# TensorE's scores moved behind the transposes in odd steps, and the additions at the end shared between two engines

## The reference

```python
h = silu(x @ W1.T + b1) @ W2.T + b2          # x: (16, 256, 128)
qkv = h @ Wg.T + bg                          # 16 heads of 64
dots = einsum('bhid,bhjd->bhij', q, k) * 64 ** -0.5
dots = where(j >= i + 64, -inf, dots)        # keys up to 63 ahead of the query
attn = softmax(dots)
out = einsum('bhij,bhjd->bhid', attn, v) -> (b, n, 1024)
x = layernorm(x + out @ Wo.T + bo)
# then: mixture of 16 experts (4 per token), add, layernorm
#       second attention (16 heads of 8), add, layernorm
#       recurrence: c = f*c + i*g over the 32 steps of 128 x 128
#       h = tanh(x @ wo.T + c_final @ uo.T + bo)
x = layernorm(x + h)                         # the end
```

## Time and profile before

| | |
|---|---|
| median of three runs | 1412.11 us |
| the profiled execution's own time | 1409.84 us |
| its span | 1408.1 us |
| mean granted TensorE clock | 0.968 |
| first attention, from the first scores to the last position | 34.3 to 669.2 us |
| experts | about 683 to 960 us |
| second attention with the recurrence | about 960 to 1379 us |
| the end (additions, norm, stores) | about 1379 to 1408 us |

### The profile page before, as it was taken

The page is one execution under the profiler, slowest core; times in us unless marked ns, Lnnn a source line. Parts: engine busy times, 40 slices in busy tenths (PEclk is TensorE's granted clock), DMA queues, the critical chain, the costliest instruction groups (busy, mean ns, idle before and its releaser), DMA issues.

```text
span 1408.1 us, 36750 instructions
## 1 busy us (share of the span) xinstructions
PE 1259.8 (89%) x9756; PEld 969.6 (69%) x9756; DVE 1016.9 (72%) x3767; ACT 928.8 (66%) x2827; POOL 774.5 (55%) x983
## 2 busy tenths in 40 slices
PE   7999999999999999995799999898687878888883
PEld 3777777777777777764699999896355555556652
DVE  1677777777777777775677777577687878878845
ACT  5877777777777877773456656464466666666554
POOL 1557777777777777775331131215446777764232
PEclk9999999999999999998799999999799999999997
DMA  9622222211222222221122222323232232323102
GB/s 338 222 61 77 74 74 74 63 46 47 74 71 71 74 74 74 74 76 46 53 71 76 80 84 81 88 78 83 62 82 70 68 84 60 88 54 75 40 2 60
DMA packets 149016, 110.98 MB, mean 79 GB/s; under 512 B 12833, under 2 KB 137249, under 8 KB 148770
## 3 DMA queue, kind: packets, MB, share of 16 engines
q1 hardware_dynamic: 139842, 92.45, 22.6%
q0 software_dynamic: 8192, 16.79, 4.4%
q10 hardware_dynamic: 864, 0.39, 0.1%
HBM read 47.27 MB, written 61.93 MB: 78 GB/s over the span
## 4 chain that ended last, share of the span: by engine, by line
PE 24%; DMA 12%; SPq 8%; DVE 5%; issue 2%; ACT 1%; DVEq 1%; ACTq 0%; POOL 0%; POOLq 0%
PE psum L917 8%; PE psum L928 8%; DMA qst<-qkd 6%; SPq L454 3%; DMA wall<-qkd 3%; DMA qkd<-parts 3%; SPq L439 2%; SPq L456 1%; PE psum L1029 1%; PE psum L905 1%; DVE parts L1603 1%; PE psum L941 1%; DVE mx L1536 1%; PE psum L981 1%; PE psum L982 1%
## 5 line engine op out<-in xcount | busy, mean ns | idle before, releaser
L555 POOL TENSOR_SCALAR P<-P,rinv 128x192 f32<-128x192 f32 (+1 forms) x384 | 309.2, 817 | 152.2 <-DVE rinv L1361 149.3
L1166 ACT ACTIVATE P<-shifted,least 128x192 f32<-128x192 f32 (+1 forms) x512 | 240.3, 471 | 107.9 <-DVE least L1345 104.6
L1188 ACT ACTIVATE hid<-psum,wA 128x128 f32<-128x128 f32 x576 | 164.5, 368 | 119.5 <-PE psum L917 119.5
L1536 DVE TENSOR_REDUCE mx<-psum 128x2 f32<-128x512 f32 x256 | 164.5, 686 | 42.1 <-PE psum L1029 34.1
L599 POOL DMA_INDIRECT yk<-xs,posc x128 | 125.0, 977 | 104.7 <-DVE wA L1497 55.4
L1196 ACT ACTIVATE wall<-psum 128x1024 f32<-128x1024 f32 x128 | 130.6, 1020 | 78.1 <-PE psum L941 77.3
L1345 DVE CUSTOM_DVE_ANT_0 shifted<-psum,band 128x192 f32<-128x192 f32 (+1 forms) x512 | 168.5, 384 | 13.1 <-PE psum L804 12.9
L917 PE MATMUL psum<-xgT,wA 128*128 128x128 f32 x1152 | 155.0, 278 | 0.6 <-DVE xgT L1504 0.6
L928 PE MATMUL psum<-wB,hid 128*128 128x128 f32 x1152 | 152.6, 276 | 0.0
L841 PEld LDWEIGHTS psum<-ident,P 128*128 128x128 f32 x1024 | 117.6, 142 | 40.1 <-issue 29.7
L917 PEld LDWEIGHTS psum<-xgT,wA 128*128 128x128 f32 x1152 | 142.8, 195 | 1.3 <-issue 0.7
(11 more groups left out here) (262 smaller groups left out, 2558.0 us busy)
## 6 DMA issues: line engine op xcount, KB each, us to landing
xs<-zrow SPq DMA_DIRECT2D x34, 1024.0 KB, 8.8
xg<-xs SPq DMA_DIRECT2D x144, 64.0 KB
xs<-yrow SPq DMA_DIRECT2D x144, 64.0 KB
wall<-in_wall SPq DMA_DIRECT2D x1, 8232.0 KB, 35.9
qkd<-parts SPq DMA_DIRECT2D x64, 96.0 KB
kst<-qkd SPq DMA_DIRECT2D x22, 128.0 KB
qst<-qkd SPq DMA_DIRECT2D x22, 128.0 KB
wall<-qkd SPq DMA_DIRECT2D x20, 128.0 KB
```

Of the source, the lines that this page charges most:

```text
L555: g.tensor_scalar(x, x, rinv[:, par, n:n + 1], None, ALU.mult).then_inc(s["pn_ready"], 1)
L1166: last = sc.activation(P[:, par, it, h, 0:w], shifted[:, par, it, h, 0:w], ACT.Exp, scale=-1.0, bias=least[:, par, n:n + 1], accum_out=row ...
L1188: sc.activation(hid[:, n % 4, f, :], up(n, f), ACT.Gelu, bias=wA[:, n % 4, F + f:F + f + 1]).then_inc(s["hid_ready"], 1)
L1536: v.tensor_reduce(out=mx[:, :, h], in_=SB[(par + 1 + h) % 3].rearrange("q (i n) -> q i n", i=TT), axis=mybir.AxisListType.X, op=ALU.max).t ...
```

## The change

In TensorE's loop the scores become a function `attend(b, p)`. In even steps it stands where it stood, first in the step. In odd steps it stands behind the transposes (and, in step 5, behind the router products), right ahead of the products with the values. No instruction is added or removed there. At the end GpSimd adds the second half of each group (`add_half`), VectorE keeps the first half; VectorE takes statistics of the first four tiles, then waits for `half_added`, then of the other four.

```diff
@@ GpSimd, the end
+            def add_half(c):
+                pool.wait_ge(s["h_act"], 2 * c + 2)
+                x, h = x_all[:, 8 * c + 4:8 * c + 8, :], xo_all[:, 8 * c + 4:8 * c + 8, :]
+                g.tensor_tensor(x, x, h, ALU.add).then_inc(s["half_added"], 1)
+
+            add_half(0)
             for c in range(GROUPS):
+                if c + 1 < GROUPS:
+                    add_half(c + 1)
                 pool.wait_ge(s["var3_ready"], c + 1)
@@ TensorE, body(b)
+            def attend(b, p):
+                need(pe, "q_ev", pair(b, p, 1))
+                need(pe, "k_ev", pair(b, p, 1))
+                need(pe, "shifted_ready", 4 * pair(b, p))
...
                 for p in range(8):
-                    if is_pair(b, p, 0):
...
+                    if p % 2 == 0 and is_pair(b, p, 0):
+                        attend(b, p)
                     if is_pair(b, p, 7):
                         qk(b, p, pair(b, p, 7))
...
                         last.then_inc(s["m_l"], 1)
+                    if p % 2 == 1 and is_pair(b, p, 0):
+                        attend(b, p)
                     if p % 2 == 1 and is_pair(b, p, -2):
@@ VectorE, squared(c)
-                for half in range(2):
-                    dve.wait_ge(s["h_act"], 2 * c + half + 1)
-                    v.tensor_tensor(x[:, 4 * half:4 * half + 4, :], ...)
+                dve.wait_ge(s["h_act"], 2 * c + 1)
+                v.tensor_tensor(x[:, 0:4, :], x[:, 0:4, :], h[:, 0:4, :], ALU.add)
                 v.drain()
-                moments(v, x, 8, st2, mv2[:, c], nh2[:, c, :], ve2[:, c, :]).then_inc(s["var3_ready"], 1)
+                statistics(v, x, 4, st2)
+                dve.wait_ge(s["half_added"], c + 1)
+                statistics(v, x[:, 4:8, :], 4, st2[:, 4:8, :])
+                variances(v, 8, st2, mv2[:, c], nh2[:, c, :], ve2[:, c, :]).then_inc(s["var3_ready"], 1)
```

More of the change, by code:

```diff
@@ L307, in build @@
             qkd_out stk zeros_out nm_ready x2_ready x2_kept x3_ready x3_kept gate_act scan_done
-            yk_in0 yk_in1 gates_in weighed comb_done var2_ready pow2_ready posc_ready xo_kept h_full fin_dve fin_pool var3_ready pow3_ready scale_ready h_act fin_ready out_done""".split()
+            yk_in0 yk_in1 gates_in weighed comb_done var2_ready pow2_ready posc_ready xo_kept h_full half_added fin_dve fin_pool var3_ready pow3_ready scale_ready h_act fin_ready out_done""".split()
         s = {n: sem(n) for n in names}
@@ L790, in _ @@
                 vproj(jt, 0, jt)
+            def attend(b, p):
+                need(pe, "q_ev", pair(b, p, 1))
+                need(pe, "k_ev", pair(b, p, 1))
+                need(pe, "shifted_ready", 4 * pair(b, p))
+                for it in range(TT):
+                    w = N - WINDOW if it == 0 else N
+                    c0 = 0 if it == 0 else N - WINDOW
+                    for h, bk in ((0, S0), (1, S1)):
+                        last = mm(bk[:, c0:c0 + w], qT[64 * h:64 * h + 64, p, it * 128:(it + 1) * 128],
+                                  kT[64 * h:64 * h + 64, p, 0:w], start=True, stop=True)
+                        if it == TT - 1:
+                            last.then_inc(s["scores"], 1)
             def body(b):
@@ L1656, in squared @@
                 x, h = x_all[:, 8 * c:8 * c + 8, :], xo_all[:, 8 * c:8 * c + 8, :]
-                for half in range(2):
-                    dve.wait_ge(s["h_act"], 2 * c + half + 1)
-                    v.tensor_tensor(x[:, 4 * half:4 * half + 4, :], x[:, 4 * half:4 * half + 4, :], h[:, 4 * half:4 * half + 4, :], ALU.add)
+                dve.wait_ge(s["h_act"], 2 * c + 1)
+                v.tensor_tensor(x[:, 0:4, :], x[:, 0:4, :], h[:, 0:4, :], ALU.add)
                 v.drain()
-                moments(v, x, 8, st2, mv2[:, c], nh2[:, c, :], ve2[:, c, :]).then_inc(s["var3_ready"], 1)
+                statistics(v, x, 4, st2)
+                dve.wait_ge(s["half_added"], c + 1)
+                statistics(v, x[:, 4:8, :], 4, st2[:, 4:8, :])
+                variances(v, 8, st2, mv2[:, c], nh2[:, c, :], ve2[:, c, :]).then_inc(s["var3_ready"], 1)
             def scales(c):
```

## The result

The changed kernel takes 1569.58 us (median of four runs, 1569.22 to 1577.01) against 1411.95 us for the kernel before on the same chip: ratio 1.1127, 95% interval 1.1085 to 1.117. It is 158 us slower. The forecast was 1549, its range 1506 to 1580: sign and range were right, and so was the mechanism in three of a batch's four turns; the size was 20 us short. The profiled execution has a span of 1567.8 us, TensorE's mean granted clock is 0.964.

What follows compares the result with a forecast made beforehand. TensorE's own work was taken to bound the first attention. Profiled execution 1409.84 + 139 (order change) - 1.7 (end) = 1547.1 us; with the median 2.3 above it, 1549, range 1506 to 1580.

Steps and rivals of the forecast that it cites:

- four turns: First attention, odd scores to next odd scores: 11.35, 13.18, 11.46 and 11.74 us, 47.73 a batch against 38.72.
- The bound before: First attention before the change: TensorE's own work sets the time, busy 38.40 of 38.72 us a batch.
- The ring: First attention: odd scores, VectorE, ScalarE, GpSimd, even pair's transposes, next odd scores wait in a circle; about +139 us.
- 47 to 48 us given as a sign: Length of a first-attention batch expected in the new profile, with TensorE busy for about 38 us.
- the plain turn: A pair of steps in the first attention without extras: hand-overs sum to 9.85 us, TensorE's own work to 9.2.
- item 2 with the second q and k product also late: Odd pair's first subtract to head 1's reciprocal, 2.41 us; lateness adds 0.4 us a turn, upper bound +165 us.
- Two thirds: Share of the added batch time taken for the first two batches, 6 us each, a choice and not a reading.
- The end: Last groups: GpSimd takes one addition per group from VectorE; -1.7 us, at most +2.5 if it holds VectorE up.
- The rival "faster": First attention: one tiling-mode edge fewer per odd step, 0.12 to 0.3 us each, 8 to 19 us gained; 1397, chance 0.06.
- The rival "clock": First attention: TensorE partly at 1.2 GHz, up to 22 us more, 1571; chance 0.08.
- "Nothing": Rival for the first attention: the waits fall just within slack, 1411 us; chance 0.02.
- "shorter turns": Rival for the first attention: the circle of waits closes, but hand-overs are at their lower bound, +100, 1510; chance 0.12.

Runs made afterwards that it cites:

- three-chain kernel: Changed kernel with ScalarE's q and k copies earlier in odd steps, GpSimd's DMAs later, VectorE's OT and PT copies for even steps earlier: 1552.78 us, ratio 1.0996.

## Why the prediction was right, point by point

- **The bound before** (TensorE's own work) fits all that was read: 0.4 us of waits in two batches. In the changed kernel TensorE is idle for 8.9 of 48.44 us, and a microsecond of added work per batch cost nothing; in the three-chain kernel 2 us cost nothing.
- **The ring.** The even pair's transposes ahead of the odd scores are what costs; this is shown by the kernel that leaves them behind the scores and comes back to 41.1 us. The four turns of a batch, predicted and measured: 11.35 and 11.41, 13.18 and 13.23, 11.46 and 11.70, 11.74 and 12.10; sum 47.73 and 48.44. That is a little over the 47 to 48 us given as a sign, and TensorE was busy for 39.51 where about 38 was given. The first two sums were right to 0.1. In the second that is partly luck: moments and reciprocal took 1.53 instead of 1.31, the norm 2.54 instead of 2.69. In the third, the second reciprocal comes later than I had read (subtract to reciprocal 3.07 instead of 2.82, 256.18 to 259.25), which is the whole 0.24. In the fourth I followed GpSimd, and ScalarE's copy of k in step 0 is later still: 0.36.
- **The step that fell short is the choice of one ring, through GpSimd, where no other work is longer.** I took it for two turns; from step 1 to 3 it held, from 7 to 1 the ring by ScalarE's copies is 0.36 longer, and the plain turn, 9.85 in the sum, is 10.0 in the three kernels where DMAs or GpSimd's link are gone, held by ScalarE's copies of the odd or the even step. That the sum came near is luck of their closeness. I had them only as an upper bound ("item 2 with the second q and k product also late"), at +0.4 a turn; it came to +0.15 to 0.36.
- **The 20 us.** Predicted span 1408.1 + 139 - 1.7 = 1545.4, measured 1567.8, 22.4 more. Turns: 14 batches x 0.71 = 9.9. The first two batches: 7.96 and 6.60 instead of 6 each, 2.6. Two thirds was too low a choice for the second; the first has a granted clock of 0.92 where the kernel before had 1.00, so what of its 2 us is the clock's stays open. The half clock in three batches (49.04, 50.49, 50.05 instead of 48.44): 4.3, less 0.5 by which two of before's (39.19 and 38.77) were over 38.72. The last batch and the drain, with half clock too, 13.2 instead of 9.0 and 0.7 and 1: 2.5. The middle, 3.7: no instruction differs there. Matched one by one, ScalarE's instructions fall back by 1.2 us where the experts start and by 1.8 us between 880 and 899 us of the kernel before, the rest in the second attention; the cause isn't shown, and the executions of the kernel before alone lie 1408.95 to 1415.72. The end: -0.2. Sum 22.3. Between the medians it is 20 and not 22, because the forecast added 2.3 for a profiled execution below its median, and the changed kernel's lies at it.
- **The end** was right: -1.9 us for -1.7. GpSimd's addition took 1.27 us, not my 1.46. The groups' powers follow after 3.44, 4.48 and 4.14 us, for 4.1 predicted. Of the contention that the Trainium skill describes ("SBUF — State Buffer", section "Who interferes with whom") the traces show one case, where VectorE's addition had begun first (1546.13) and the power second (1546.30): the power took 2.02 us, the others 1.64 to 1.65. Two further powers (1549.74 and 1554.22) began ahead of VectorE's additions (1550.69 and 1554.85) and ran beside them, and neither took longer: the additions took 0.69 and 0.68. So the traces agree with the section in the first order alone, where the second one took 0.37 us longer; in the other order nobody was held up. It cost nothing, so the upper bound of +2.5 was too wide.
- **The rival "faster"** stays small or nothing, and open in size. Scores and products with the values take the same time from start to start as before (0.96 and 1.66 us). The q and k product takes 0.97 us behind scores. Behind transposes it nearly always waits a little now and takes 0.93 to 0.97; in the few places of the first attention where it doesn't (two in the changed kernel, four each in the one with added work and the one with GpSimd's transfers moved) it takes 0.87. That comes near my lower value of 0.12 per odd step, 7 us in all; where TensorE waits 8.9 us per batch it is worth nothing.
- **The rival "clock"** was underrated in kind. In the changed kernel it cost some 5 us, not 22. In the three-chain kernel it cost about 2.7 us in every batch but the first ones. The Trainium skill, "TensorE: Matmul & The Clock Gate", section "A second HAM failure mode: psum-queue depth-cycling", tells of a kernel whose small idle times between groups made the clock go back and forth; the traces here agree so far that the clock falls although no single wait of TensorE in the steady batches is over 2 us. That the waits are the cause they don't show.
- **"Nothing"** and **"shorter turns"** are out: no turn was shorter than summed.

## What to carry to other kernels

Before moving an instruction in one in-order queue, follow it round all the others: if what it now stands behind depends on what the same instruction released one turn ago, the two make a ring, and the sum of single hand-overs in a timeline gives its length to a few per cent. Add up the second and third chain too; a wait is worth only the lead of its chain over the next, and nothing where a later wait in the same turn ends last. And where an engine that set the time has been made to wait, look at its granted clock before explaining the rest by dependencies.

## What the runs showed of the hardware

- The same instructions of the same program took 45.02 us a batch, and from one batch to the next 47.80, because TensorE's clock fell to 1.2 GHz at the same place of each batch from then on, for 6.8 us in the rows shown. It went on to the end of the stage. What made it fall isn't shown.
- Work added to TensorE made a kernel faster: 1552.78 and 1529.43 us with none and sixteen extra transposes per batch. With eight (1545.58) two of four executions were faster and two were not.
- Executions of these two kernels lay 15 and 26 us apart, the slow ones at the lower granted clock: 1538.49 us at 0.953 and 1553.1 at 0.940 with eight, 1521.47 at 0.961 and 1547.84 at 0.940 with sixteen.
- Moving scores next to products with the values, so that a half-array group follows a half-array group, changed the time of neither from start to start.
